# Softmax attention on one core: the second pass' scores ordered one position earlier, preparation spread out, and the bf16 splits on GpSimd

## What is computed

```
q, k, v = heads(x @ Wq.T), heads(x @ Wk.T), heads(x @ Wv.T)     # x after a layer norm
sim = q k^T / sqrt(8), causal
probs = softmax(sim);  entropy = -sum(probs * log(probs + 1e-9))
beta = where(entropy > 0.5, max(poly4(entropy), 1), 1)
out = softmax(sim * beta) @ v;   x = x + out @ Wo.T + bo
```

## Time and profile before

| | us |
|---|---|
| median of 3 runs | 2694.11 (2691.54 to 2702.1) |
| the profiled execution, its own time | 2696.02 |
| its span | 2694.2 |
| busy: PE / DVE / ACT / POOL | 1694.7 / 1548.0 / 1393.0 / 73.8 |

### The profile page before, as it was taken

The page is one execution under the profiler, slowest core; times in us unless marked ns, Lnnn a source line. Parts: engine busy times, 40 slices in busy tenths (PEclk is TensorE's granted clock), DMA queues, the critical chain, the costliest instruction groups (busy, mean ns, idle before and its releaser), DMA issues. The chain is left out here.

```text
span 2694.2 us, 23532 instructions
## 1 busy us (share of the span) xinstructions
PE 1694.7 (63%) x6573; PEld 748.6 (28%) x6573; DVE 1548.0 (57%) x3577; ACT 1393.0 (52%) x2650; POOL 73.8 (3%) x71
## 2 busy tenths in 40 slices
PE   3544554899999944477777787677877642122172
PEld 2222332344444420122223222232222210111141
DVE  3444343445353449987788777977777134477411
ACT  2222222434343319888988999898989531000020
POOL 0000000000000010000000000000000000000314
PEclk9666666999999975566667656776667875555586
DMA  3000000555555510110101010201010100100212
GB/s 119 0 0 0 0 0 0 137 152 133 145 141 144 153 51 25 35 70 21 59 19 75 19 60 18 84 18 56 23 55 7 43 3 12 24 0 0 91 62 74
DMA packets 55812, 143.38 MB, mean 53 GB/s; under 512 B 7640, under 2 KB 22648, under 8 KB 53088
## 3 DMA queue, kind: packets, MB, share of 16 engines
q1 hardware_dynamic: 53648, 137.84, 17.3%
q0 software_dynamic: 2048, 4.20, 0.5%
HBM read 124.56 MB, written 17.45 MB: 53 GB/s over the span
## 5 line engine op out<-in xcount | busy, mean ns | idle before, releaser
L1273 DVE CUSTOM_DVE_ANT_0 sa_lg<-sa_e,sa_lg 128x1024 f32<-128x1024 f32 (+7 forms) x512 | 387.0, 756 | 162.6 <-ACT sa_lg L1185 162.6
L1053 PE MATMUL sa_ps<-sa_k1s,sa_q1s 72*128 72x512 bf16 (+3 forms) x768 | 297.2, 456 | 233.6 <-DVE sa_nmax L1264 197.0
L1175 ACT ACTIVATE sa_e<-sa_e,sa_nmax 128x1024 f32<-128x1024 f32 (+7 forms) x512 | 401.3, 784 | 48.6 <-DVE sa_nmax L1264 48.3
L1264 DVE CUSTOM_DVE_ANT_0 sa_e<-sa_ps,sa_mask 128x1024 f32<-128x1024 f32 (+7 forms) x512 | 385.3, 753 | 36.6 <-PE sa_ps L1053 34.9
L1185 ACT ACTIVATE sa_lg<-sa_e,sa_sum 128x1024 f32<-128x1024 f32 (+7 forms) x512 | 400.6, 782 | 2.7 <-DVE sa_prod L1273 2.2
L1193 ACT ACTIVATE sa_p<-sa_ps 128x512 f32<-128x512 f32 x576 | 336.5, 601 | 110.1 <-PE sa_ps L1087 55.8
L1084 PE MATMUL sa_ps<-sa_q2s,sa_k2s 75*128 75x512 bf16 (+3 forms) x768 | 299.9, 428 | 91.7 <-ACT sa_p L1193 70.1
L701 DVE TENSOR_TENSOR mx_hw<-mx_spread,mx_h 128x512 f32<-128x512 f32 x256 | 176.3, 691 | 252.2 <-ACT mx_h L608 242.5
L608 ACT ACTIVATE mx_h<-mx_ps 128x512 f32<-128x512 f32 (+1 forms) x264 | 156.7, 596 | 286.0 <-PE mx_ps L544 277.7
L544 PE MATMUL mx_ps<-mx_f,m 128*128 128x512 f32 x512 | 263.0, 595 | 1.7 <-ACT mx_h L608 1.7
L557 PE MATMUL mx_ps<-mx_hw,m 128*128 128x512 f32 x512 | 262.0, 594 | 1.7 <-DVE mx_hw L701 1.7
(11 more groups left out here) (287 smaller groups left out, 1952.4 us busy)
## 6 DMA issues: line engine op xcount, KB each, us to landing
mx_spread<-mx_spill SPq DMA_DIRECT2D x256, 256.0 KB, 4.0
sa_q1s<-sa_spill_q SPq DMA_DIRECT2D x96, 96.0 KB
sa_k1s<-sa_spill_k SPq DMA_DIRECT2D x96, 96.0 KB
sa_q2s<-sa_spill_q SPq DMA_DIRECT2D x48, 192.0 KB
sa_k2s<-sa_spill_k SPq DMA_DIRECT2D x48, 192.0 KB
m<-m_in SPq DMA_DIRECT2D x1, 4256.0 KB, 16.0
be_w<-w_in SPq DMA_DIRECT2D x16, 256.0 KB, 6.1
sa_spill_q<-sa_qp SPq DMA_DIRECT2D x4, 768.0 KB, 13.3
```

The lines of the kernel that those rows point to most:

```text
L1053: last = nc.tensor.matmul(out[:, col:col + w], q_ring[:, c % 2, local, i * P:(i + 1) * P], k_ring[:, c % 2, local, col:col + w], start=Tru ...
L1175: nc.scalar.activation(e[:, u % 5, 0:w], e[:, u % 5, 0:w], ACT.Exp, scale=-1.0, bias=nmax[:, b % 2, i, h:h + 1], accum_out=sums[:, b % 2, ...
L1264: nc.vector.tensor_tensor_reduce(out=e[:, u % 5, 0:w], in0=slot_of("unit", u)[:, 0:w], in1=mask_wide[:, SEQ - w:SEQ], scale=1.0, scalar=3. ...
L1273: nc.vector.tensor_tensor_reduce(out=lg[:, u % 2, 0:w], in0=e[:, u % 5, 0:w], in1=lg[:, u % 2, 0:w], scale=1.0, scalar=0.0, op0=ALU.mult, ...
```

## The change

1. On TensorE the loop over `second` and `answer` moves up, right behind `score(u + AHEAD)`, and takes the pieces of position u + 1 instead of u.
2. The preparation of the next sequence moves from positions 75 to 97 to positions 13 to 53; the v projection stays at 106.
3. The splits of q, k and q×beta leave VectorE and become a program of GpSimd, each step of it chained to the one before by a semaphore. `take_k` on VectorE keeps the first copy and subtraction, which read PSUM, and waits for GpSimd's `q_split` as it waited for its own. The split of q×beta gets a tile of its own, `sa_left2`.

```diff
-        A_AT, Q_AT, K_AT, V_AT = 83, 86, 88, 106
+        A_AT, Q_AT, K_AT, V_AT = 23, 33, 44, 106
# SyncE
-                    if (b := batch_at(u, 92)) is not None:
+                    if (b := batch_at(u, 43)) is not None:
                         spill_first("q", b, q_split, q_parts, spill_q, q_spilled)
-                    if (b := batch_at(u, 97)) is not None:
+                    if (b := batch_at(u, 53)) is not None:
                         spill_first("k", b, k_split, k_parts, spill_k, k_spilled)
# GpSimd
+                def link(ins):
+                    made[0] += 1
+                    ins.then_inc(pool_chain.sem, 1)
+                    pool.wait_ge(pool_chain.sem, made[0])
+                def split_rest(rest, out, done):
+                    link(nc.gpsimd.tensor_copy(out[1], rest))
+                    link(nc.gpsimd.tensor_tensor(rest, rest, out[1], ALU.subtract))
+                    nc.gpsimd.tensor_copy(out[2], rest).then_inc(done.sem, 1)
+                def split_q(b):
+                    ...
+                    link(nc.gpsimd.tensor_copy(out[0], q_cm[b % 2][:, :]))
+                    link(nc.gpsimd.tensor_tensor(left, q_cm[b % 2][:, :], out[0], ALU.subtract))
+                    split_rest(left, out, q_split)
+                def split_k(b):
+                    pool.wait_ge(k_read.sem, b + 1)
+                    split_rest(left, [k_parts[:, k, :] for k in range(PARTS)], k_split)
+                def split_q2(k):
+                    ...
+                    pool.wait_ge(wide_read.sem, k + 1)
+                    ...
+                    link(nc.gpsimd.tensor_copy(out[0], q[rows, :]))
+                    link(nc.gpsimd.tensor_tensor(left2[rows, :], q[rows, :], out[0], ALU.subtract))
+                    split_rest(left2[rows, :], out, q2_split)
+                split_q(0)
+                split_k(0)
+                for u in range(END):
+                    if (k := side_at(u, 8)) is not None:
+                        split_q2(k)
+                    if (b := batch_at(u, Q_AT + 1)) is not None:
+                        split_q(b)
+                    if (b := batch_at(u, K_AT + 1)) is not None:
+                        split_k(b)
# TensorE
                     if u + AHEAD < ALL1:
                         score(u + AHEAD)
+                    for m in pieces2_at(u + 1):
+                        second(m)
+                        if m % GROUP == GROUP - 1 and m >= GROUP:
+                            answer(m // GROUP - 1)
...
-                    for m in pieces2_at(u):
-                        second(m)
-                        if m % GROUP == GROUP - 1 and m >= GROUP:
-                            answer(m // GROUP - 1)
# ScalarE
-                    if (b := batch_at(u, 77)) is not None:
+                    if (b := batch_at(u, 16)) is not None:
+                        act.wait_ge(k_split.sem, b)
                         ln.square(nc, act, b, 1)
-                    if (b := batch_at(u, 79)) is not None:
+                    if (b := batch_at(u, 18)) is not None:
                         ln.root(nc, act, b, 1, load=False)
# VectorE: split_q2, split_q, split_k gone; norm steps from 75, 76, 78, 80 to 13, 14, 17, 20
```

More of the change, by code:

```diff
@@ L861, in softmax_attention_block @@
         left = buffers[2][:, :, :].rearrange("p t c -> p (t c)")
+        left2 = sb("sa_left2", [P, SEQ])
         a_cm = sb("sa_a", [P, SEQ])
@@ L899, in softmax_attention_block @@
         att_t, att_copied, o_mm, x_ready = sig("sa_att_t"), sig("sa_att_c"), sig("sa_o"), sig("sa_xr")
-        chain = sig("sa_chain")
+        chain, pool_chain = sig("sa_chain"), sig("sa_pool_chain")
         ident = mat(m1, MATS1, "ident")
@@ L1010, in _ @@
                 nc.gpsimd.memset(values[:, :, :, :, HEAD:HEAD + 1], 1.0).then_inc(ready.sem, 1)
+                made = [0]
+                def link(ins):
[7 more added lines that the diff above has]
+                def split_q(b):
+                    out = [q_parts[:, k, :] for k in range(PARTS)]
+                    pool.wait_ge(q_ready.sem, b + 1)
+                    if b:
+                        pool.wait_ge(q_spilled.sem, 16 * b)
+                    link(nc.gpsimd.tensor_copy(out[0], q_cm[b % 2][:, :]))
[5 more added lines that the diff above has]
+                def split_q2(k):
+                    rows, q = rows_of(k), q_cm[k // 2 % 2]
+                    out = [q2_parts[rows, j, :] for j in range(PARTS)]
+                    pool.wait_ge(wide_read.sem, k + 1)
+                    if k >= 2:
+                        pool.wait_ge(q2_spilled.sem, 16 * (k - 1))
+                    link(nc.gpsimd.tensor_copy(out[0], q[rows, :]))
[10 more added lines that the diff above has]
+                        split_k(b)
             @block.tensor
@@ L1142, in _ @@
                         score(u + AHEAD)
+                    for m in pieces2_at(u + 1):
+                        second(m)
+                        if m % GROUP == GROUP - 1 and m >= GROUP:
+                            answer(m // GROUP - 1)
+                    if group_at(u, 2) == ALL_GROUPS - 1:
+                        answer(ALL2 - 1)
                     if (k := side_at(u, WIDE_AT)) is not None:
@@ L1312, in widened @@
                                             ).then_inc(wide_read.sem, 1)
[L1314 to L1320, removed]
                 def take_a(b):
@@ L1338, in take_k @@
                     nc.vector.tensor_tensor(left, src, out[0], ALU.subtract).then_inc(k_read.sem, 1)
[L1339 to L1349, removed]
                 def take_v(b):
@@ L1398, in _ @@
                 take_q(0)
-                split_q(0, range(5))
                 take_k(0)
-                split_k(range(2, 5))
                 dve.wait_ge(ready.sem, 3)
@@ L1420, in _ @@
                         widened(k)
[L1421 to L1424, removed]
+                    if (b := batch_at(u, 13)) is not None:
                         ln.total(nc, seq(b))
-                    if (b := batch_at(u, 76)) is not None:
+                    if (b := batch_at(u, 14)) is not None:
                         ln.subtract(nc, dve, b, 1, seq(b))
-                    if (b := batch_at(u, 78)) is not None:
+                    if (b := batch_at(u, 17)) is not None:
                         ln.variance(nc, dve, b, 1)
-                    if (b := batch_at(u, 80)) is not None:
+                    if (b := batch_at(u, 20)) is not None:
                         ln.scale(nc, dve, b, 1, y_tm[:, :, :])
```

9 lines of the change are left out of this document (removed).

## The result

The changed kernel took 2722.8 us in the median, the kernel before 2698.0 beside it: ratio 1.0094, interval 1.0074 to 1.0114, slower by 0.9%. The forecast was 2665, its range ended at 2702. The profiled executions spanned 2719.5 and 2694.2 us, 25.3 apart. Three runs in this document fell in a slower state of the chip and are left out of medians and ratios: two of e7's twelve and one of the kernel before beside it.

A forecast was written before the change was run, and what follows sets the result against it. ScalarE was taken to set the pace where both passes run, with its idle time to be gained. Terms 7.7 + 7 − 2.7 − 23.3 − 22 + 3.6 = −29.7 us gave 2665 us against the median, range 2630 to 2702.

The forecast's parts named there:

- Stretches between: Seven stretches from group start to ahead of the next widening: 33.6 us idle, 8 left with the lead; net −22 us.
- the lead does not help: Rival: next position's second waits for exp2 and holds back score, idle time between sides stays; 2686 us, chance 0.05.
- First 64 positions: First pass alone: sequence 1's preparation moves in, 9.8 us of VectorE against 3.7 us left; +7 us.
- contention rival: GpSimd and VectorE's product hinder each other: split 12.8 us in the stream, 6 us in first 64 positions; 2695, chance 0.20.
- Start: Stage start before position 0: slower q and k splits on GpSimd plus 2 us for an ISA instruction; +7.7 us.
- Price of a split: GpSimd's split of three copies and two subtractions: 8.3 us alone, 9.3 us inside the stream.
- sides: Six later sides, widening to group start: the split's chain becomes the bound at 31.4 us each; −23.3 us.
- first side: From the end of the first widened to the first second-pass score: 34.1 us becomes 31.4; −2.7 us.
- tail: After the last widening nothing hides GpSimd's split, which becomes 8.3 us; +3.6 us.
- Slow split: Rival: GpSimd's split so slow, 15 us, that it holds every group start, the start and tail; 2722 us, chance 0.13.

The follow-up runs named there:

- e7: e3 plus six more casts and six more subtractions on GpSimd behind each of the eight q2 splits, with no one waiting for them: 2699.7 us, ratio 1.0009.
- e3: The changed kernel with the loop of second-pass scores back at its old place and position (no lead): 2689.2 us, ratio 0.9968.
- e5: The changed kernel with the loop of second and answer back at its old place, still one position ahead: 2694.3 us, ratio 0.9990.
- e2: The kernel before with only the preparation, takes and spills moved to the new positions, all splits on VectorE: 2703.5 us, ratio 1.0032.
- e8: The kernel before with only the q2 splits on GpSimd, with a tile of their own: 2685.0 us, ratio 0.9946.

## Why the prediction was wrong

**Stretches between, −22: the failed step.** I wrote that with a position of lead I leave 8 of the 33.6 us of idle time. It measured +22.2; without the lead (e3) the same stretches take 4.9 us less than before. The step took the lead as a gift to ScalarE and never asked what stands behind the waiting `second` on TensorE: turns, projections, `widen`, the shift. They came late by the wait, the second-pass scores and the answers, and VectorE, in order, held both passes (7.6 us at the turns before, 52.5 after). At the turns the wait is the smaller part, 0.5 of 2.9 us, and the `answer` that the lead moved ahead of them the larger, 1.8. e5 shows that with this work put back ahead of the loop the lead costs 5 us instead of 34; even then it gains nothing between the sides (732.2 us, 730.8 before).

**Rival "the lead does not help"** had the right wait and a tenth of the weight it needed: it let the gain vanish (2686) where it became a loss, and named only `score` as held back. "TensorE has 230 us without work" was no argument against it, since an engine that waits at the head of its list does nothing behind it: the turns came 2.9 us late with that idle time there.

**First 64 positions, +7:** measured +16.7, and 19.1 with the splits on VectorE (e2). Busy time from the first score to the end of the first `widened`, before and after (columns as in the earlier trace rows):

```profile
1004.03:1115.32 111.29, 48.96 (x127) 12.00 (x127) 104.55 (x306) 104.58 (x219) 0.00 (x0) 0.51 0.07 27
1007.41:1135.36 127.95, 58.92 (x143) 16.41 (x143) 118.23 (x314) 107.76 (x222) 13.79 (x8) 0.50 0.09 35
```

VectorE's work grew by 13.7 us: 9.0 are the added steps, as priced, and 4.8 are the product, which took 58.2 us instead of 53.5. The term had nothing for that; the contention rival had 6. And I had set 3.7 us of VectorE's slack against the added work. That slack was not taken up: VectorE's idle time rose from 6.7 to 9.7 us. In e2, where GpSimd does nothing, the product stayed at 53.4, the added steps and splits were 15.9, and the idle time was 10.0. What the idle time waits for was not taken apart.

**Start, +7.7:** +3.4. The 2 us for the extra instruction were nothing, the splits were 1.1 us shorter than priced, and the stage itself began 1.4 us earlier in this run. The Trainium skill, GPSIMD Engine Reference, section Instruction dispatch, has a load of about 6 us at the first call of freshly loaded code; here the first cast and the first subtraction begin 0.06 and 0.08 us behind what they wait for, and no such load shows.

**Price of a split, sides, first side, tail:** right within 0.6, 2.1, 0.4 and 0.1 us. The chain took 31.5 to 31.9 us on all six sides, against 31.4. But the reason given for the sides, that the lead frees ScalarE of 4.3 us there, was not needed: without the lead e3's six sides take 192.2 us, 1.6 more. GpSimd's split, 9.3 us instead of 12.3, and the moved preparation make that gain; the preparation alone gave 6.2 (e2), the splits of q2 alone 13.0 (e8).

**Contention rival:** present, but not as written. GpSimd's split was not stretched to 12.8 us but to 9.3; most of the price fell on VectorE's product. The Trainium skill, GPSIMD Engine Reference, section Key points, names this contention; the trace agrees (below), and e7 shows that about a fifth of it reaches the end.

**Slow split:** excluded by the 7.66 us. That 2722 came out is not its doing.

## What to carry to other kernels

Before an instruction that can wait is moved ahead on an in-order engine, list everything that then stands behind it and who waits for each; the short jobs that feed another in-order engine belong ahead of it. A shift by one position also changes which jobs share a position: here every turn came to stand behind an `answer`. Idle time of the engine is no cover where it lies ahead of the wait. And changes that come together are worth taking apart: here one third of the change (the splits of q2) gained half a per cent, and the rest hid it.

## What the hardware showed

VectorE's product, with two inputs in SBUF, is slowed while GpSimd works, and `evacuate`, with one input in PSUM, is not (753 ns mean before and after, 751 in e7). In the changed kernel's timeline a product of 128x896, 1.09 us elsewhere, takes 2.60 beside a subtraction of GpSimd, whose next cast, begun before the product ended, takes 1.78 instead of 1.04:

```profile
1069.03 2.13 POOL L1031 TENSOR_TENSOR sa_sq<-sa_q,sa_qp 128x1024 f32<-128x1024 f32 x1
1069.50 2.60 DVE L1320 CUSTOM_DVE_ANT_0 sa_lg<-sa_e,sa_lg 128x896 f32<-128x896 f32 x1
1071.22 1.78 POOL L1021 CAST sa_qp<-sa_sq 128x1024 bf16<-128x1024 f32 x1
```
